# First norm and routing of a fused MoE, attention, MoE kernel: gate weights on ScalarE's queue, later fills, another interleaving

## The reference, cut to what matters

```python
x = x + 0.5 * _L0_ffn_ref(_layernorm(x), w_gate, b_gate, W1, b1, W2, b2)
x = x + _L0_attn_ref(_layernorm(x), norm_w, Wq, bq, Wk, bk, Wv, bv, Wo, bo)
x = x + 0.5 * _L0_ffn_ref(_layernorm(x), w_gate, b_gate, W1, b1, W2, b2)
# _L0_ffn_ref:
logits = x_flat @ w_gate + b_gate          # 8 experts
probs = softmax(logits); route_p = max(probs); route_idx = argmax(probs)
h = relu(x_flat @ W1[e] + b1[e]); y = h @ W2[e] + b2[e]
out = y[route_idx] * route_p               # one expert for each token
```

## Time and profile before

| | us |
|---|---|
| median of 3 runs (353.55 to 354.95) | 354.32 |
| profiled execution, its own time | 352.22 |
| profiled execution, span | 350.5 |
| first instruction to the last scatter's start | 39.39 |
| first expert product | 45.36 |
| TensorE busy, share of the span | 72% |

### The profile page before, as it was taken

How to read it: one execution, slowest core, us unless ns; L and a number is a source line. 1 busy time by engine, 2 the same in 40 slices (tenths; PEclk the granted TensorE clock), 3 DMA queues, 4 the chain that set the end, 5 groups by cost and what they waited for, 6 DMA issues and landing times.

```text
span 350.5 us, 7325 instructions
## 1 busy us (share of the span) xinstructions
PE 253.5 (72%) x2094; PEld 184.7 (53%) x2094; DVE 225.2 (64%) x691; ACT 139.9 (40%) x330; POOL 177.3 (51%) x304
## 2 busy tenths in 40 slices
PE   0660099999318557699999999999776305999980
PEld 0650089999314333345555555554543305999970
DVE  5885048887365887467676677676764471888760
ACT  3410034444114640266666657677431101444420
POOL 7757405454546741246665565556447640354452
PEclk9999999999957995599999999999965555999996
DMA  7957232332040636744222122110001264033300
GB/s 207 411 200 226 95 104 72 106 90 83 6 120 0 180 106 207 228 141 137 62 68 61 46 62 69 57 48 4 2 32 64 87 182 122 25 100 106 104 20 1
DMA packets 34753, 35.40 MB, mean 101 GB/s; under 512 B 3964, under 2 KB 28673, under 8 KB 34720
## 3 DMA queue, kind: packets, MB, share of 16 engines
q1 hardware_dynamic: 29984, 27.07, 25.5%
q0 software_dynamic: 3008, 6.34, 5.5%
q10 hardware_dynamic: 1728, 1.59, 1.6%
HBM read 20.05 MB, written 15.65 MB: 102 GB/s over the span
## 4 chain that ended last, share of the span: by engine, by line
PE 52%; POOL 13%; DMA 9%; issue 8%; DVE 7%; SPq 7%; ACT 1%; POOLq 0%; DVEq 0%; ACTq 0%
PE bank L1167 12%; PE bank L1178 10%; POOL disp_d L455 6%; PE bank L1280 5%; PE bank L1306 4%; SPq L376 3%; PE bank L1256 3%; PE bank L1303 3%; DMA xs_sb<-disp_d 2%; POOL rs L447 2%; PE bank L1286 2%; DMA disp_d<-row,slot 2%; PE bank L1253 2%; PE bank L1322 2%; PE bank L1159 2%
## 5 line engine op out<-in xcount | busy, mean ns | idle before, releaser
L671 ACT ACTIVATE pT<-bank 128x512 f32<-128x512 f32 x96 | 57.3, 597 | 49.8 <-PE bank L1280 26.5
L968 DVE TENSOR_REDUCE mh<-bank 128x2 f32<-128x512 f32 x64 | 44.1, 689 | 16.4 <-PE bank L1256 15.9
L533 POOL TENSOR_SCALAR_AFFINE_SELECT pT<-pT 128x512 f32<-128x512 f32 x64 | 40.6, 635 | 27.3 <-ACT pT L671 26.8
L1167 PE MATMUL bank<-xsT,ew 128*128 128x128 f32 x368 | 51.6, 286 | 0.1
L1178 PE MATMUL bank<-experts,hT 128*128 x368 | 48.7, 276 | 0.0
L1167 PEld LDWEIGHTS bank<-xsT,ew 128*128 128x128 f32 x368 | 47.5, 202 | 0.6 <-issue 0.3
L862 DVE TENSOR_SCALAR hT<-bank,ew 128x128 f32<-128x128 f32 x92 | 28.0, 346 | 27.8 <-PE bank L1167 26.7
L1178 PEld LDWEIGHTS bank<-experts,hT 128*128 128x128 f32 x368 | 44.8, 192 | 0.3 <-issue 0.3
L609 ACT ACTIVATE hT<-bank,ew 128x128 f32<-128x128 f32 x92 | 28.7, 363 | 32.8 <-PE bank L1167 32.8
L455 POOL DMA_INDIRECT disp_d<-row,slot x32 | 31.6, 988 | 18.7 <-issue 8.3
L463 POOL DMA_INDIRECT out<-ys_sb,xs_sb x23 | 22.5, 980 | 33.3 <-DVE ys_sb L886 32.7
(11 more groups left out here) (126 smaller groups left out, 446.1 us busy)
## 6 DMA issues: line engine op xcount, KB each, us to landing
sp_d<-spl SPq DMA_DIRECT2D x32, 192.0 KB, 2.9
xs_sb<-disp_d SPq DMA_DIRECT2D x46, 129.0 KB, 2.2
experts<-in_experts SPq DMA_DIRECT2D x8, 578.0 KB, 8.8
qz<-sp_d SPq DMA_DIRECT2D x32, 96.0 KB
ks<-sp_d SPq DMA_DIRECT2D x32, 96.0 KB
disp_d<-pad ACTq DMA_DIRECT2D x12, 129.0 KB, 3.5
row<-in_x SPq DMA_DIRECT2D x4, 256.0 KB, 4.0
row<-x_d SPq DMA_DIRECT2D x4, 256.0 KB, 3.8
```

What stands on the lines that cost most here:

```text
L533: pool.affine_select(out=p_, in_=p_, pattern=[[0, 4], [1, P]], compare_op=ALU.is_ge, fill=0.0, base=0, channel_multiplier=-1).then_inc(a_p ...
L671: act.activation(pT[:, u, :], bank[2 + u % 2][:, :], ACT.Exp, scale=SCALE).then_inc(a_e, 1)
L968: dve.tensor_reduce(mh[:, half, 1, :, 2 * pp + w], bank[u % 2][:, :].rearrange("p (h n) -> p h n", h=2), AX.X, ALU.max).then_inc(a_mx, 1)
L1167: mm = pe.matmul(bank[2 + 2 * (k % 2) + c // 2][:, (c % 2) * P:(c % 2 + 1) * P], ew[:, k % WRING, c * P:(c + 1) * P], xsT[:, k % 2, :], st ...
```

## The change

The loads of `wg`, the gate bias and `cst` go from SP's queue to ScalarE's, at the start of its program. The gate bias has a small buffer of its own, and `rows` now counts with the attention's weights. The constant -0.5 is written by GpSimd. TensorE no longer pairs turns: it goes turn, logits, turn, logits, and waits for `cb` (the bfloat16 constants) only ahead of ranks 0. ScalarE and VectorE are interleaved otherwise: routing of chunk 0 starts ahead of the last two quads' apply. GpSimd's `stack_fill(1)` and the fills of `va` move behind the 16 scatters.

```diff
             for q in range(NQ):
                 sp.dma_start(x[:, 4 * q:4 * q + 4, :], xv[:, 4 * q:4 * q + 4, :]).then_inc(x_in_s[q], 16)
-                if q == 0:
-                    sp.dma_start(cst[:, :], const_in).then_inc(cst_s, 16)
-            sp.dma_start(wg[:, :], w_gate).then_inc(gate_s, 16)
-            sp.dma_start(rows[:, :], rows_in.partition_broadcast(P)).then_inc(gate_s, 16)
+            sp.dma_start(rows[:, :], rows_in.partition_broadcast(P)).then_inc(attw_s, 16)
# GpSimd
+            pool.memset(mhalf[:, :], -0.5).then_inc(zero_s, 1)
             stack_fill(0)
-            pool.wait_ge(cst_s, 16)
-            ln_scale(0, 0)
-            ln_scale(0, 1)
+            pool.wait_ge(zero_s, 2)
+            for q in range(NQ):
+                ln_scale(0, q)
+            pool.wait_ge(ids_s, 1)
+            for c, (t0, t1, _, _, _) in enumerate(CHUNK[0]):
+                dispatch(0, c, range(t0, t1))
             stack_fill(1)
-            ln_scale(0, 2)
-            ln_scale(0, 3)
             pool.memset(va[:, :, :, :, :], 0.0).then_inc(static_s, 1)
             pool.wait_ge(static_s, 5)
             pool.memset(va[:, :, :, :, HD:HD + 1], 1.0).then_inc(static_s, 1)
-            pool.wait_ge(ids_s, 1)
-            for c, (t0, t1, _, _, _) in enumerate(CHUNK[0]):
-                dispatch(0, c, range(t0, t1))
# ScalarE
+            act.dma_start(wg[:, :], w_gate).then_inc(gate_s, 16)
+            act.dma_start(b_gate[:, :], rows_in[3 * D:3 * D + NE].partition_broadcast(P)).then_inc(gate_s, 16)
+            act.dma_start(cst[:, :], const_in).then_inc(cst_s, 16)
+            ln_apply(0, 0)
+            gate_copy(0, 0)
             act.wait_ge(cst_s, 16)
             act.copy(cb[:, :], cst[:, 0:C_J]).then_inc(cb_s, 1)
-            for q in range(NQ):
-                ln_apply(0, q)
-                gate_copy(0, q)
-                if q == 2:
-                    route_exp(0, 0)
+            ln_apply(0, 1)
+            gate_copy(0, 1)
+            route_exp(0, 0)
+            ln_apply(0, 2)
+            gate_copy(0, 2)
+            ln_apply(0, 3)
+            gate_copy(0, 3)
             route_exp(0, 1)
             route_exp(0, 2)
# VectorE
             ln_stats(0, 0)
-            for q in range(1, NQ):
-                ln_stats(0, q)
-                ln_bias(0, q - 1)
-                ln_apply(0, q - 1)
-            ln_bias(0, NQ - 1)
-            ln_apply(0, NQ - 1)
+            ln_stats(0, 1)
+            ln_bias(0, 0)
+            ln_apply(0, 0)
+            ln_stats(0, 2)
+            ln_bias(0, 1)
+            ln_apply(0, 1)
+            ln_stats(0, 3)
             dve.wait_ge(cst_s, 16)
+            dve.tensor_copy(row[:, :, ID].bitcast(U32), cst[:, C_IDS:C_IDS + NT]).then_inc(ids_s, 1)
+            dve.wait_ge(pad_s, 1)
+            dve.tensor_copy(pad[:, ID:ID + 1].bitcast(U32), cst[:, C_PAD:C_PAD + 1]).then_inc(pad_s, 1)
             dve.wait_ge(gate_s, 32)
             route_pick(0, 0)
-            dve.tensor_copy(row[:, :, ID].bitcast(U32), cst[:, C_IDS:C_IDS + NT]).then_inc(ids_s, 1)
+            ln_bias(0, 2)
+            ln_apply(0, 2)
             route_slot(0, 0)
+            ln_bias(0, 3)
+            ln_apply(0, 3)
             route_pick(0, 1)
             route_slot(0, 1)
-            dve.wait_ge(pad_s, 1)
-            dve.tensor_copy(pad[:, ID:ID + 1].bitcast(U32), cst[:, C_PAD:C_PAD + 1]).then_inc(pad_s, 1)
             route_pick(0, 2)
# TensorE
-            pe.wait_ge(cb_s, 1)
-            pe.wait_ge(gate_s, 32)
-            gate_turn(0, 0)
-            gate_turn(0, 1)
-            logits(0, 0)
+            gate_turn(0, 0)
+            pe.wait_ge(gate_s, 32)
+            logits(0, 0)
+            gate_turn(0, 1)
+            logits(0, 1)
+            pe.wait_ge(cb_s, 1)
+            ranks(0, 0)
             gate_turn(0, 2)
-            logits(0, 1)
-            ranks(0, 0)
-            gate_turn(0, 3)
             logits(0, 2)
             ranks(0, 1)
+            gate_turn(0, 3)
             logits(0, 3)
             ranks(0, 2)
```

More of the change, by code:

```diff
@@ L70 @@
 C_ID, C_UP, C_MS, C_ONE, C_J, C_REV, C_BASE, C_PADR = 0, 128, 256, 384, 512, 528, 536, 544
-C_MHALF = C_PADR + NE
-C_T = C_MHALF + 4
+C_T = C_PADR + NE
 C_ROW = C_T + NS
@@ L89, in constants @@
     c[:, C_PADR:C_PADR + NE] = CAP * np.arange(NE) + 1 - REGIONS
-    c[:, C_MHALF:C_MHALF + 4] = -0.5
     c[:, C_T:C_T + NS] = np.arange(NS)
@@ L126, in build @@
         norm_w, bv, bo = (rows[:, i * D:(i + 1) * D] for i in range(3))
-        b_gate = rows[:, 3 * D:3 * D + NE]
+        b_gate = sb("b_gate", [P, NE])[:, :]
+        mhalf = sb("mhalf", [P, 4])
         st6 = sb("st6", [P, NT, 6])
@@ L446, in ln_scale @@
                 pool.wait_ge(ln_vs[n], q + 1)
-                pool.tensor_tensor(rs[:, ts], vs[:, ts], cst[:, C_MHALF:C_MHALF + t1 - t0], ALU.pow
+                pool.tensor_tensor(rs[:, ts], vs[:, ts], mhalf[:, 0:t1 - t0], ALU.pow
                                    ).then_inc(ln_rs[n], 1)
@@ L634, in _ @@
             expert_tiles(0)
-            act.wait_ge(attw_s, 32)
+            act.wait_ge(attw_s, 48)
             def quad_copy(q):
@@ L934, in _ @@
             tile_table(0)
-            dve.wait_ge(attw_s, 32)
+            dve.wait_ge(attw_s, 48)
             dve.tensor_scalar(wt[:, 0:3, :], wt[:, 0:3, :], cols[:, 2:3], None, ALU.mult).then_inc(w_nw, 1)
```

## The result

The changed kernel takes **351.19 us** (median of 20 runs, 348.99 to 353.65) against 353.39 for the kernel before (20 runs): 2.2 less, a ratio of 0.9938 with a 95% interval of 0.9915 to 0.996. The profiled execution took 351.21, its span 349.4. The forecast was 352.4 with 1.9 saved.

The account below looks back on a forecast made before the run. The prediction took GpSimd's scatter chain, released by slots 0 to 2, to bound the touched stage. 2.1 at the last scatter less 0.2 for loads saves 1.9: 354.3 to 352.4, range 350.9 to 354.3 (own 351.8 to 353.0).

Parts of the forecast that it names:

- The frame: Routing stage: the change is worth exactly the time by which GpSimd's last scatter starts earlier, 39.39 to 37.3.
- A later release caps the gain: GpSimd's scatters: first 3.05 earlier, but fifth (slot 1) and ninth (slot 2) only 2.1; slot 2's spare 3.34 decides.
- TensorE's serial order costs back the early start: TensorE: turn, copy and logits in series, 3.70 a quad; last logits end at 22.6 against 22.47, early start gone.
- Fills: GpSimd's fills stretched VectorE's apply by 1.9, covered before but not in the new order; behind the scatters they cost 0.
- Turn 0 at 7.5: TensorE's first turn starts at 7.5 instead of 10.19, so its chain gains 2.65.
- What pulls the other way: Loads of gate weights, bias and constants beside x: 0.2 for the first stats, 0 for quad 1 (bound 0.3).
- GpSimd's own pace: Rival, chance 0.15: slots 1 and 2 come in time, all 3.05 of slot 0 stay, 351.3.
- Early start lost on the way in: Rival, chance 0.22: late constants or slowed x delay turn 0; with 1.3 lost, 0.8 is left, 353.5.
- The slower case: Rival, chance 0.08: constants release TensorE's serial chain late; turn 0 at 12.0 gives 2.4 more, 356.7.
- The gain does not reach the end: Rival without a chance of its own: waits in the rest of the kernel absorb the earlier last scatter.

Follow-up runs that it names:

- apply 0 first: Two kernels, VectorE's bias and apply of quad 0 ahead of quad 1's stats, chunk 1's exponential ahead of the last gate copy: changed kernel 0.9893, all loads on SP 0.9889.
- fills alone: Kernel before with only the fills moved behind the 16 scatters: ratio 1.0012 to the kernel before, last scatter 39.26.
- fills back: Changed kernel with the fills at their old places: last scatter 38.25 against 37.40, ratio 0.9899 to the kernel before.
- one-queue kernel: Changed kernel with all loads on SP's queue, gate bias still its own buffer: last scatter 36.73, ratio 0.9901 to the kernel before.
- loads-back kernel: Changed kernel with all loads as before (one queue, constants second, gate bias inside broadcast rows): last scatter 37.17, ratio 0.9917 to the kernel before.
- loads alone: Kernel before with only the loads moved and -0.5 written by GpSimd: last scatter 39.83, ratio 0.9979 to the kernel before.

## Why the prediction was right, and where it was not

**The frame held.** The worth is what the last scatter gains: 1.99 there, 2.2 in the medians, 1.9 forecast. In the table, ratios follow the last scatter only roughly: the intervals are some 0.7% wide, 2.4 us, and can't order kernels whose scatters lie within 1 us. What is said of such differences below rests on the traces.

**A later release caps the gain**: right, and it is the step that mattered, but the release that does it is slot 1, as in the prediction's own list, and not slot 2, whose spare time it says "decides". The start at TensorE was 1.07 later than forecast and the first scatter 0.8 later (17.69 for 16.9); the fifth waited for slot 1 and was only 0.15 later (23.25 for 23.1). So the scatters gained 2.24 at the first, 1.97 at the fifth and 1.98 at the ninth. Slot 2 held no scatter in the changed kernel. In the two kernels with apply 0 first, the ninth scatter starts 0.81 behind the end of slot 2 (26.92 to 27.73, 26.21 to 27.02), about the shortest that any release was seen to take: there its spare time is gone.

**TensorE's serial order costs back the early start**: right. The quads follow at 3.55 where the forecast had 3.70 once and 3.82 twice, and the chain takes 2.0 more in all than with the old overlap (14.30 against 12.29).

**Fills**: right in both halves. Their clash was covered before (fills alone: 39.26), would not be covered in the new order (fills back: 0.85), and behind the scatters they are free.

**Turn 0 at 7.5** was wrong by 1.07 (8.57), and this is the step that failed: "What pulls the other way". I took 0.2 for the first stats and 0 for quad 1. The first stats came at 3.91; but with the old loads they came anywhere from 3.52 to 3.77, so at most part of the 0.37 is the change's. Quad 1, forecast at 5.0, came at 6.18, beyond my bound of 0.3.

The gate bias is the term that was mis-sized. I priced the two gate loads at 0.4 by the second stretch of the earlier trace rows, as if its small packets made the traffic fall to 251 GB/s. That reading was wrong: in the microsecond behind it the small packets are nearly gone, only 11 are left, and the traffic is lower still. What runs there, by the order of the queue, is `rows`, the broadcast of one 2 KB row to 128 partitions.

```profile
DMA packets 89, 0.16 MB, mean 160 GB/s; under 512 B 11, under 2 KB 11, under 8 KB 89
```

In the changed kernel the two gate loads run mostly one behind the other: `wg` lands at 3.5, the bias at 5.9. These are 2.5 to 3.5 and 3.5 to 5.5 us:

```profile
DMA packets 735, 0.29 MB, mean 294 GB/s; under 512 B 170, under 2 KB 735, under 8 KB 735
```
```profile
DMA packets 702, 0.32 MB, mean 158 GB/s; under 512 B 145, under 2 KB 688, under 8 KB 702
```

Against the 329 GB/s of the earlier trace rows, the first stretch lost 0.04 MB and the second 0.34 MB, which is an estimated 0.1 and 1.0 us of all the DMA engines' time. Both loads are 4 KB for 128 partitions; `wg` has 128 rows of its own, the bias reads one row of 32 bytes 128 times. So the cost goes with the broadcast and not with the number or size of the packets. This is read from two loads at different moments; no run changed the broadcast alone. In the one-queue kernel the microsecond with 304 small packets, of both gate loads, moved 163 GB/s after 356: 0.19 MB less, near 0.55, and there it fell behind quad 1.

**It came out right with some luck.** Two errors met the late start. The serial chain was 0.8 shorter in all than forecast, so of the 1.07 only 0.27 was left at the last logits (22.87 for 22.6). And slot 1 released its scatter in 0.78 (22.47 to 23.25) and not in 0.9. At the last scatter 0.1 was left (37.40 for 37.3). The 0.2 that I took off for the loads was thus not what the loads cost, and the forecast of 1.9 met the 1.99 by errors that cancelled.

**The loads' part in it I had not asked about.** The prediction counts 2.65 of early start and names the gate's loads as what held TensorE. It did not see that the new order alone takes that wait off turn 0. The loads-back kernel shows it: orders and fills (with -0.5 written by GpSimd) give all of the gain. With the old orders the loads did count, beside the fills: 0.98.

**Rivals.** The median, 351.19, is nearest to the 351.3 of "GpSimd's own pace"; the trace decides against it. Slot 0 did not bring 3.05 but 2.24, and 0.27 of wait is left ahead of the fifth scatter. "Early start lost on the way in" did happen, in size 1.07, but the wait for slot 1 took most of it up. The slower case did not come; constants as the release of turn 0 were met once, with apply 0 first, at 8.21. "The gain does not reach the end" is not borne out by the medians (2.2), though in the two profiled executions only 1.0 of it is seen; the last section has what lies between.

## What to carry to other kernels

Price an early start at each release of the chain behind it, and not at the first; here the forecast had 3.05 at the first scatter and 2.1 at the last, and the trace 2.24 and 1.99. Two waits that end together hide each other, so an edit that is worth nothing alone can be worth a microsecond beside another, and orders of several engines have to be changed together. Before a load is moved to be earlier, look whether its wait merely stands in front of work that does not need it: moving the wait was enough here, and the second queue took bandwidth from the loads that were needed first. When a small load is priced, ask what it reads and not only how many packets it has.

## What the runs showed of the hardware

**Slow products in the first expert tiles.** Rows of the changed kernel's TensorE, and the windows of the slow stretch (busy time of PE, PEld, DVE, ACT, POOL; granted clock; DMA share; GB/s):

```profile
45.10 1.91 PE L1174 MATMUL bank<-xsT,ew 128*128 128x128 f32 x8
46.80 1.52 PE L1185 MATMUL bank<-experts,hT 128*128 x8
...
48.27 1.06 PE L1174 MATMUL bank<-xsT,ew 128*128 128x128 f32 x8
```
```profile
45.00:46.00 1.00, 1.00 (x7) 1.00 (x6) 0.61 (x2) 0.78 (x3) 0.00 (x0) 1.00 0.68 189
46.00:47.00 1.00, 1.00 (x6) 1.00 (x6) 0.00 (x0) 0.00 (x0) 0.00 (x0) 1.00 0.00 0
```

TensorE stood idle for 16.7 until the first expert transpose at 42.18. The same eight products then take 1.91 at 45.10 and 1.06 at 48.27, while the granted clock reads 1.00, that is 2.4 GHz, in all of it. DMA traffic alone does not explain it: the products at 46.80 are still slow (1.52, later 1.06), and from 46 to 48 no DMA runs. The slow stretch from the first expert transpose lasted some 4 in the profile of before (43.98 to 47.9), 6 in the changed kernel (42.18 to 48.1), 4 with one queue (41.49 to 45.6) and 6 with the loads alone (44.52 to 50.5). The idle time before it (18.8, 16.7, 16.7 and 19.0) does not sort them, and the cause stays open. In line with it, the first result scatter stood 13.4 behind the last token scatter before and 14.2 after. That is 0.8 of the gain, and the two profiled executions differ by only 1.0 where the medians differ by 2.2. The Trainium skill ("TensorE: Matmul & The Clock Gate", Part 1) says that the number of slow products at the start differs between runs of one kernel; the traces agree with such a spread, though each is of another kernel, and the page's warning that clock events in a trace are not always reliable fits the column that reads 1.00.

**A broadcast load is dear for its size.** The gate bias, 32 bytes read 128 times, had 158 GB/s of traffic beside it for two microseconds, and `rows`, 2 KB read 128 times, ran at 160; `wg`, with as many packets as the bias, ran with 294. The broadcast was not varied alone.

**A scatter's release and pace.** Where GpSimd waits for a slot, its scatter starts 0.78 to 0.98 behind the slot's end, the 0.97 to 0.98 after the long waits for slot 0 and the 0.78 to 0.79 after the short ones for slot 1. Behind another scatter it is idle for 0.30.

**ScalarE's table load** did not go ahead of the three DMA issues: it ran from 2.42 for 1.28, in front of the wait of the first apply, and cost nothing.
